# Staging moved into the q and k stage, q and k with four blocks interleaved, and another order of the engines' work around the last u

## The reference

```python
def _L0_tok_ref(x, qkv_w, qkv_b, proj_w, proj_b):        # windows of 8 x 8 tokens, 8 heads of 8
    ...
    q = _rope2(q.reshape(-1, WH, WW, hd)).reshape(-1, NH, N, hd)
    k = _rope2(k.reshape(-1, WH, WW, hd)).reshape(-1, NH, N, hd)
    attn = jax.nn.softmax(q * scale @ jnp.swapaxes(k, -2, -1), axis=-1)
    out = (attn @ v).transpose(0, 2, 1, 3).reshape(-1, N, C)
    ...
    return out @ proj_w.T + proj_b

def _selective_scan(u, delta, A, Bm, Cm, D):
    deltaA = jnp.einsum('bld,dn->bldn', delta, A)
    deltaBu = jnp.einsum('bld,bld,bln->bldn', delta, u, Bm)
    shifted = jnp.concatenate([deltaA[:, 1:], jnp.zeros_like(deltaA[:, :1])], axis=1)
    cum = jnp.exp(jnp.flip(jnp.cumsum(jnp.flip(shifted, axis=1), axis=1), axis=1))
    x = jnp.cumsum(deltaBu * cum, axis=1) / (cum + 1e-12)
    return jnp.einsum('bldn,bln->bld', x, Cm) + u * D

h = _L0_tok_ref(x, ...)
h = h + _L0_attn_ref(_layernorm(h, axis=-1), ...)   # u is the layernorm, delta = softplus(u W)
h = h + _L0_ffn_ref(_layernorm(h, axis=-1), ...)    # the expert with the largest logit
```

## Time and profile before

| | us |
|---|---|
| median of 3 runs | 658.89 (656.12 to 661.49) |
| the profiled execution | 659.24 |
| its span | 657.2 |
| TensorE busy | 566.3 (86%) |
| VectorE busy | 526.6 (80%) |
| ScalarE busy | 404.3 (62%) |
| Pool busy | 308.4 (47%) |

### The profile page before, as it was taken

The page is one execution under the profiler, slowest core; times in us unless marked ns, Lnnn a source line. Parts: engine busy times, 40 slices in busy tenths (PEclk is TensorE's granted clock), DMA queues, the critical chain, the costliest instruction groups (busy, mean ns, idle before and its releaser), DMA issues. The chain is left out here.

```text
span 657.2 us, 18275 instructions
## 1 busy us (share of the span) xinstructions
PE 566.3 (86%) x7079; PEld 385.3 (59%) x7080; DVE 526.6 (80%) x943; ACT 404.3 (62%) x659; POOL 308.4 (47%) x352
## 2 busy tenths in 40 slices
PE   3795499999999999999955666649999999999995
PEld 3331388888888888888721222235555555555552
DVE  3898389999889999989669899957777777777762
ACT  3696267767777777777759556504555555555543
POOL 5401234555555565555299759853433333332420
PEclk9899599999999999999967888978999999999998
DMA  9500222223322222221000000000011010101001
GB/s 194 84 1 9 61 56 51 54 55 65 72 57 55 51 56 52 59 55 28 2 0 1 0 0 0 2 1 10 21 22 23 21 24 20 25 19 23 22 21 25
DMA packets 62376, 23.01 MB, mean 35 GB/s; under 512 B 45778, under 2 KB 62290, under 8 KB 62290
## 3 DMA queue, kind: packets, MB, share of 16 engines
q1 hardware_dynamic: 61472, 21.69, 16.1%
q10 hardware_dynamic: 690, 0.13, 0.1%
q0 software_dynamic: 128, 0.00, 0.0%
HBM read 5.02 MB, written 4.19 MB: 14 GB/s over the span
## 5 line engine op out<-in xcount | busy, mean ns | idle before, releaser
L602 ACT ACTIVATE work<-work 128x1024 f32<-128x1024 f32 x64 | 67.7, 1057 | 66.3 <-DVE work L666 66.3
L661 DVE TENSOR_REDUCE work<-psum 128x16 f32<-128x1024 f32 x64 | 78.0, 1219 | 30.1 <-PE psum L502 30.1
L469 POOL TENSOR_TENSOR work<-work 128x4 f32<-128x4 f32 x32 | 34.3, 1072 | 105.3 <-DVE work L703 105.3
L517 PE MATMUL psum<-kc,work 128*128 128x128 f32 x512 | 75.2, 280 | 8.9 <-DVE work L678 7.8
L666 DVE TENSOR_TENSOR work<-psum,work 128x1024 f32<-128x1024 f32 x64 | 78.3, 1224 | 2.2
L1724 ACT ACTIVATE hid<-psum,b1c 128x512 f32<-128x512 f32 x96 | 58.9, 684 | 33.3 <-PE psum L1631 33.3
L610 ACT ACTIVATE work<-psum 128x512 f32<-128x512 f32 x128 | 71.0, 591 | 6.4 <-PE psum L517 4.9
L1639 PE MATMUL psum<-x_t,w1x 64*64 64x256 f32 x1024 | 71.7, 396 | 0.0
L517 PEld LDWEIGHTS psum<-kc,work 128*128 128x128 f32 x512 | 58.4, 143 | 17.4 <-DVE work L678 15.5
L1614 POOL TENSOR_TENSOR m_sq<-m_xc 128x256 f32<-128x256 f32 x32 | 19.6, 612 | 101.5 <-DVE m_xc L1775 101.5
L533 PEld LDWEIGHTS psum<-work 128*64 128x64 f32 x2048 | 62.3, 138 | 6.2 <-ACT work L610 6.0
(11 more groups left out here) (192 smaller groups left out, 1260.1 us busy)
## 6 DMA issues: line engine op xcount, KB each, us to landing
work<-big_bc SPq DMA_DIRECT2D x256, 32.0 KB, 2.0
h_all<-in_x SPq DMA_DIRECT2D x16, 256.0 KB, 5.2
work<-big_a SPq DMA_DIRECT2D x32, 128.0 KB, 2.2
out<-out_st SPq DMA_DIRECT2D x128, 32.0 KB
w1x<-in_L_ffn_W SPq DMA_DIRECT2D x2, 128.0 KB, 4.3
kc<-constants SPq DMA_DIRECT2D x1, 202.0 KB, 2.9
w2x<-in_L_ffn_W SPq DMA_DIRECT2D x1, 128.0 KB, 3.2
wraw<-in_L_tok_qkv_w ACTq DMA_DIRECT2D x2, 32.0 KB, 3.6
```

The lines of the kernel that those rows point to most:

```text
L469: pool.tensor_tensor(rstd[:, :], var[:, :], mhalf[:, :], ALU.pow).then_inc(rstd_done, 1)
L517: m = pe.transpose(banks[4 + half][:, n * P:n * P + P], prob[:, f, at:at + 2, :], ident)
L602: act.activation(prob[:, f], prob[:, f], ACT.Exp).then_inc(prob_done, 1)
L661: dve.tensor_reduce(top[:, f, :].rearrange("p (g h) -> p g h", g=4), sc, AX.X, ALU.max).then_inc(top_done, 1)
```

## The change

First, q and k lie differently in `qkT`: the four windows of a group are interleaved, window innermost. `copy_qk` therefore writes runs of four words (eta 1) or of 32 (eta 0) and reads PSUM with a step of eight words. `mask_qk` reads `raw` with a step of four words and writes `k_st` and `q_st` as before. The transfers have the same shapes.

Second, staging moves into the first block. One buffer `work` is now there in both blocks, and the first block's own tiles lie in the part of it that the attention uses later. SP fetches q and k of groups 0 and 1 and x of group 0 as soon as the first half of q and k is written. Pool writes the zeros and ones of `v_st` and masks group 0.

Third, work around the end of attention changes places: Pool's constants go ahead of group 18; ScalarE does below(2) and grown(2) ahead of the last u copy; VectorE's product `wide` moves behind suffix(2); `low` is made with tensor_scalar instead of tensor_tensor; TensorE loads the flags behind spread(2).

```diff
+            work = stages.enter_context(nc.sbuf_tensor("work", [P, 9456], F32))
+            take = carve(work)
+            at = dict(kc=kc, xT=xT, qkT=qkT, raw=take([P, 2, 2, WIN, 4]), x_st=take([P, 2, 2, WIN]),
+                      q_st=take([P, 2, 2, P]), k_st=take([P, 2, 2, 2, WIN]), v_st=take([P, 2, 4, 2, 4, 18]),
...
+            sb1 = carve(work, 3456)
...
-                dst = qkT[q, qk, half * L:half * L + L].rearrange("p (s r c) -> p s r c", r=8, c=8)
-                dst = dst[:, :, :, v] if eta else dst[:, :, v, :]
+                dst = qkT[q, qk, half * L:half * L + L].rearrange("p (i r c s) -> p i r c s", r=8, c=8, s=4)
+                dst = dst[:, :, :, v, :] if eta else dst[:, :, v, :, :]
                 eng.wait_ge(qk_done, m + 1)
-                src = banks[4 + m % 4][q, :].rearrange("p (s c) -> p s c", c=8)
+                src = banks[4 + m % 4][q, :].rearrange("p (i s c) -> p i c s", s=4, c=8)
...
+                    sp.wait_ge(qk_act, 16)
+                    sp.wait_ge(qk_dve, 16)
+                    for i in range(2):
+                        fetch_qk(sp, at, i)
+                    fetch_x(sp, at, 0)
...
+                    v_st = at["v_st"]
+                    pool.memset(v_st[:, :, :, :, :, :], 0.0).then_inc(at["v_zeroed"], 1)
...
+                    pool.wait_ge(at["qk_staged"][0], 128)
+                    mask_qk(pool, at, 0)
...
+def mask_qk(pool, t, i):
+    kc, raw = t["kc"], t["raw"]
+    wide = [P, 4, 2, WIN]
+    head, win = (kc[:, at:at + 2].unsqueeze(1).unsqueeze(3).broadcast_to(wide) for at in (K_HEAD, K_WIN))
+    q, k = (raw[:, i % 2, n].rearrange("p k s -> p s k").unsqueeze(2).broadcast_to(wide) for n in range(2))
+    pool.tensor_tensor(t["k_st"][:, :, :, :, :].rearrange("p f b h k -> p (f b) h k"), k, head, ALU.mult
+                       ).then_inc(t["k_masked"], 1)
...
+            if live(i, -1) and i >= 1:
+                sp.wait_ge(k_masked, i)
+                sp.wait_ge(q_masked, i)
+                fetch_qk(sp, t, i + 1)
+            if live(i, 0) and i >= 1:
                 sp.wait_ge(v_done, i * 2)
+                fetch_x(sp, t, i)
...
-            if live(i, -2):
-                masks(i + 2, par)
+            if live(i, -2) and i >= -1:
+                pool.wait_ge(qk_staged[par], (i + 2) // 2 * 128 + 128)
+                pool.wait_ge(scores_done, i * 4 + 8)
+                mask_qk(pool, t, i + 2)
...
             pe.wait_ge(delta_done, 7)
-            for p in range(1, 8):
+            for p in range(1, 3):
+                spread(p)
+            alive_of, some = flags(pe)
+            for p in range(3, 8):
                 spread(p)
...
+                if i == QUADS + 3:
+                    below(2)
+                    grown(2)
...
             att["act"](act, ahead, amid)
-            for k in range(2, 7):
+            logged(2)
+            for k in range(3, 7):
...
             dve.memset(segments.rearrange("p (r t) -> p r t", t=TAIL)[:, :, 0], 0.0).then_inc(seg_set, 1)
+            for k in range(1, 3):
+                delta(k)
+                suffix(k)
             dve.tensor_tensor(wide[:, :, 0], u_tail[:, 0].unsqueeze(1).broadcast_to([P, 2 * NS, TAIL]),
                               wd[:, RANK:].unsqueeze(2).broadcast_to([P, 2 * NS, TAIL]), ALU.mult).then_inc(wide_set, 1)
-            for k in range(1, 4):
-                delta(k)
-                suffix(k)
+            delta(3)
+            suffix(3)
...
-                dve.tensor_tensor(low[:, m:m + 1], later[:, last:last + 1], later[:, L + last:L + last + 1],
+                dve.tensor_scalar(low[:, m:m + 1], later[:, last:last + 1], later[:, L + last:L + last + 1], None,
```

More of the change, by code:

```diff
@@ L369, in attention @@
     ident = kc[:, K_IDENT:K_IDENT + P]
-    raw = take([P, 2, 2, 4, WIN])
-    x_st = take([P, 2, 2, WIN])
-    q_st = take([P, 2, 2, P])
-    k_st = take([P, 2, 2, 2, WIN])
     top = take([P, 2, 16])
@@ L376, in attention @@
     prob_t = take([P, 2, 8, P])
-    v_st = take([P, 2, 4, 2, 4, 18])
     inv = take([P, 32])
@@ L451, in run_pool @@
         pool.wait_ge(power_set, 1)
-        def masks(i, par):
-            pool.wait_ge(qk_staged[par], i // 2 * 128 + 128)
-            if not first(i):
-                pool.wait_ge(scores_done, i * 4)
-            wide = [P, 4, 2, WIN]
-            head, win = (kc[:, at:at + 2].unsqueeze(1).unsqueeze(3).broadcast_to(wide) for at in (K_HEAD, K_WIN))
-            q, k = (raw[:, par, n].unsqueeze(2).broadcast_to(wide) for n in range(2))
-            pool.tensor_tensor(k_st[:, :, :, :, :].rearrange("p f b h k -> p (f b) h k"), k, head, ALU.mult
-                               ).then_inc(k_masked, 1)
-            pool.tensor_tensor(q_st[:, :, :, :].rearrange("p f b (w k) -> p (f b) w k", w=2), q, win, ALU.mult
-                               ).then_inc(q_masked, 1)
         def body(i, par):
@@ L716, in raster, with carve @@
                    dep_tracking_offset=a.dep_tracking_offset)
-def attention_and_scan(nc, t, moe, out):
-    with ExitStack() as ctx:
-        def sb(name, shape, dt=F32):
-            return ctx.enter_context(nc.sbuf_tensor(name, shape, dt))
-        t["w1x"] = sb("w1x", [P, NE, HID])
-        t["w2x"] = sb("w2x", [P, 4, C])
-        t["b1c"] = sb("b1c", [P, 4])
-        t["b2p"] = sb("b2p", [96, C], BF16)
-        t["b2r"] = sb("b2r", [96, C])
-        t["rw"] = sb("rw", [NE, 2, C])
-        t["rwx"] = sb("rwx", [P, 2, NE])
-        t["rb_row"] = sb("rb_row", [P, NE])
-        with ExitStack() as scan_ctx:
-            both_stages(nc, scan_ctx, t, moe)
-        experts(nc, ctx, t, out)
-def carve(work):
-    used = [0]
+def carve(work, start=0):
+    used = [start]
     def take(shape):
@@ L752, in carve, with both_stages @@
     return take
-def both_stages(nc, ctx, t, moe):
+def both_stages(nc, ctx, t, work, moe):
     router_w, router_b, w1, b1, w2, b2 = moe
@@ L972, in _ @@
             mine = (b_done, c_done)
-            alive_of, some = flags(pe)
             with pe.If(alive_of[0][0] > 0):
```

143 lines of the change are left out of this document (71 added, 72 removed).

## The result

The changed kernel took 640.12 us in the median of 4 runs (639.99 to 640.38), the kernel before 658.43 (4 runs, 656.12 to 661.49): a ratio of 0.973, with a 95% interval of 0.970 to 0.976. The forecast was 641.0, and its range 636.5 to 651.5. The profiled execution took 639.99, its span is 637.9. The total was met to 1 us; the parts were not, and that is what the rest is about.

A forecast was written before the change was run, and what follows sets the result against it. Evictions were taken to pace the first block, staging to stall attention's start, TensorE and VectorE to be nearly full afterwards. Terms -3.5 - 9.7 - 2.0 - 1.6 - 1.5 = -18.3 from 659.24 gave 641 us, range 636.5 to 651.5.

The forecast's parts named there:

- The evictions: First block, q and k copied out of PSUM: single-word reads free, 0.74 us each, TensorE's pace decides; -3.5 us.
- Rival 1: First block: single-word PSUM reads cost like such writes, evictions bring +1.2 to +6.0; total 646.4 to 651.3 us; chance 0.27.
- The staging: Start of second block: transfers and first masks already done, VectorE's first reduction 1.4 us behind instead of 11.1; -9.7 us.
- the step that a shorter pause of TensorE keeps the clock up: Start of second block: TensorE's pause shrinks to some 2 us, first scores at high level; -9.7 rather than -8.9 us.
- Rival 4: End of first block: evictions stretch SP's issue, staging not ready, second block 6.5 us later; 647 us; chance 0.04.
- The masks and the constants: Pool in attention: masks up to 0.7 us dearer per group and constants before group 18 both fit its waits; 0.
- The last u: End of attention: power takes 1.01 us with the product moved, z(3) and delta(3) come sooner; -2.0 us.
- rival 2: Around the last u: moved product or `low` still waits for Pool, 3.6 us less gain; 644.5 us; chance 0.08.
- `low`: End of attention, VectorE: as tensor_scalar its two instructions take about 0.15 us each, the first no longer 1.845; -1.6 us.
- The flags: Before the first b matmuls: early loading removes 2.09 us of TensorE issue, for which VectorE waits 1.49; -1.5 us.

The follow-up runs named there:

- x2: The changed kernel with only the old layout of q and k (single-word writes, contiguous reads of `raw`): 643.74 us, ratio 0.979 to the kernel before.
- x1: The changed kernel run again with no edit, as reference on the experiments' chip: 641.49 us, ratio 0.976 to the kernel before.
- x3: The changed kernel with transfers of groups 0 and 1, x and the first masks back in the second block: 650.59 us, ratio 0.989 to the kernel before.
- x10: The changed kernel with two more mask-sized Pool products ahead of every group's masks: 663.34 us, ratio 1.008 to the kernel before.
- x0: The kernel before, unedited, profiled a second time: 657.38 us, span 655.3.
- x4b: The changed kernel with VectorE's product `wide` back directly behind the last variance: 644.16 us, ratio 0.978 to the kernel before.
- x9: The changed kernel with one more mask-sized Pool product ahead of every group's masks: 643.57 us, ratio 0.978 to the kernel before.

## Why the prediction was right, and where it was not

**The evictions (foreseen -3.5).** Right in mechanism. Reads of single words from PSUM are free: 750 ns on VectorE and 682 on ScalarE, as much as the row evictions took with contiguous reads (0.74 and 0.68). With the low stretch of before in it, I had the last eviction 28.7 us behind the first (57.0 less 28.33). It came after 26.97, exactly the 1.7 us less that I had added for four half steps at 1.2 GHz, which this execution did not have. Between x2 and x1, at the same clock, the layout is worth 4.2. Rival 1 (646.4 to 651.3), the one with 0.27, is out. By the Trainium skill, "Vector Engine (DVE) Microarchitecture Reference", section 5.2, this part would have cost 1.2 us by my estimate; its table is of SBUF, and the trace shows that it does not carry over to PSUM reads.

**The staging (-9.7).** -9.66, and 10.07 when undone. Rival 4 is out: everything had landed 2.4 us before the block began. But the step that a shorter pause of TensorE keeps the clock up was half wrong. The first scores did run at the high level (1.17). The pause that brings the clock down is the next one, at 58.6 to 63.8 us, which I had not looked for, because in before the low level was already there when group 0 ran. That cost 2.6 us in the second cycle, in the four executions that have the long low stretch and not in the others, and it is the miss that the total hides. I had allowed the first cycle to fall from 9.0 to 7.6; it fell only with TensorE kept busy.

**The masks and the constants (0).** Right as to the time. A mask costs 25% more (1.30 against 1.04), between my bounds. By the Trainium skill, "GPSIMD Engine Reference", section 7, it would be 50% more; the trace shows half of that. The slack behind the masks was 2.5 less 0.5, measured as 1.95. The constants are hidden with 0.21 us left.

**The last u (-2.0).** -2.4, so rival 2 is out. I had delta(3) at 342.4 on the clock of before, 10.4 us behind the variance. Seven other executions have exactly that, 10.40, with delta(3) waiting 0.34 for ScalarE. In after it was 10.01: the last copy of u came 0.25 sooner and z(3) was for the most part at the higher level (5.35 us). The moved product then waited 0.3 for Pool, not 0.1, and delta(3) started as it ended.

**`low` (-1.6).** -1.58, though not for the reason that the sum names. With the old form at the new place only 0.2 of the 1.6 come back. So most of it comes from the place: `low` no longer stands behind a Pool instruction that has just begun. The new form at the old place, beside such an instruction, was not run.

**The flags (-1.5).** The step that failed, although this segment fell by 1.56. I took the 2.09 us of issue for the whole cause of VectorE's wait of 1.49, since they stood next to each other. The b matmuls behind the gap ran at 1.2 GHz (3.59 us for four), and without that there is no such wait: behind the same gap, VectorE did not wait at all in the second execution of before, where they ran at 2.4 GHz, and 0.27 us with the flags put back, where one of four did not. In these the edit is worth 0 to 0.3; the 1.5 are there only when the low level falls on those matmuls, as in the first execution of before. And with the flags early the same 1.6 us were lost in x3 and x10, at the spreads. A second profile of the kernel before would have shown it ahead of time.

**The sum.** That the total came within 1 us is in part luck. Against the second execution of before the span fell by 17.4: -5.4 in the first block, -9.7, +2.6, -2.4, -1.6, and -1.1 before the first eviction. The forecast of -18.3 held because its two misses (2.6 forgotten, 1.5 promised by the flags) met two terms that came out larger and a start that was earlier.

## What to carry to other kernels

Before a wait beside TensorE is charged to an instruction, compare its matmuls with the same ones elsewhere: if they take twice as long, the clock has a part in the wait, and another execution may not have it. When work is moved out of a stall, look for TensorE's next pause; a few matmuls that nothing reads, in a place where it waits anyway, won 3.3 us of 641 here. Slack is measured by spending it: one more instruction per group that left the cycle at 7.61 us and a second that made it 8.26 tell more than the busy share.

## What the runs showed of the hardware

- Reading PSUM at one word in eight cost nothing: 750 ns on VectorE and 682 on ScalarE for 64 x 512 fp32 (0.74 and 0.68 with contiguous reads), where writing single words to SBUF took 1.15 to 1.18 us.
- A Pool product with one operand of 128 x 512 read at a step of four words took 1.30 us instead of 1.04.
- A power of four elements per partition on Pool took 3.03 us when VectorE's product of two SBUF tensors had begun 0.15 us before it (before, x0, x4b), and 1.01 elsewhere. The other way round, a VectorE instruction of one column with two SBUF tensors took 0.47 and 1.85 us instead of 0.15 and ended with Pool's instruction in flight. As tensor_scalar, with one tensor and a scalar from SBUF and its result in PSUM, two took 0.33 beside such a Pool instruction.
- At the start of the second block the 1.2 GHz level came while TensorE was nearly idle (busy 0.88 of the 4 us from 60 on), and lasted 6.8 us in some executions (x9) and 13.6 in others (after), with TensorE's instructions at the same times up to there. Where and how long it comes differs between executions of one kernel. It changed the first segment by up to 2.0 us, the three groups by 2.6, the segment to the first full block by 1.6 and the expert stage by 1.3, as much as several of the terms of this sum.
